# W_base turned and split during the attention periods and kept in DRAM, in a two-part transformer block on one core

## What is computed

```python
mod = (_silu(c) @ wmod).reshape(2, 6, 1, -1)
sa, ca, ga, sb, cb, gb = ...
h = layernorm(x) * (1 + ca) + sa
x = x + ga * attention(h, wq, wk, wv, wo)
h = layernorm(x) * (1 + cb) + sb
base = einsum('bsd,od->bso', h, W_base) + b_base
moe = experts(h, W_gate, W_thr, b_thr, A_w, B_w)
x = x + gb * (base + moe)
```

## Time and profile before

| | before |
|---|---|
| median of 3 runs | 1817.67 us |
| the profiled execution: time / span | 1819.76 / 1818.0 us |
| TensorE matmul busy | 1643.7 us (90%) |
| VectorE / ScalarE / GpSimd busy | 1010.9 / 985.4 / 611.1 us |
| mean DMA rate | 96 GB/s |
| chain that ended last: TensorE / ScalarE / VectorE / issue / DMA | 63 / 10 / 10 / 8 / 4% |

### The profile page before, as it was taken

How to read it: one execution, slowest core, us unless ns; L and a number is a source line. 1 busy time by engine, 2 the same in 40 slices (tenths; PEclk the granted TensorE clock), 3 DMA queues, 4 the chain that set the end, 5 groups by cost and what they waited for, 6 DMA issues and landing times.

```text
span 1818.0 us, 29711 instructions
## 1 busy us (share of the span) xinstructions
PE 1643.7 (90%) x9459; PEld 1196.8 (66%) x9459; DVE 1010.9 (56%) x3248; ACT 985.4 (54%) x2368; POOL 611.1 (34%) x483
## 2 busy tenths in 40 slices
PE   3667989999999998899999999999879999999997
PEld 0235666666666765677667667666457888888885
DVE  1535547667576664556666666665535445445443
ACT  1333667887887776667777777777742101101110
POOL 1441424334343230423433332331322333333342
PEclk8788999999999998999999999998589999999998
DMA  9633233444443338223323323223443211211210
GB/s 338 226 135 76 74 86 91 108 122 109 129 114 77 97 77 247 57 61 96 72 68 97 71 68 97 67 60 78 119 132 93 70 59 45 70 49 56 69 48 34
DMA packets 170786, 174.52 MB, mean 96 GB/s; under 512 B 20898, under 2 KB 120562, under 8 KB 170644
## 3 DMA queue, kind: packets, MB, share of 16 engines
q1 hardware_dynamic: 166484, 164.42, 32.5%
q10 hardware_dynamic: 4160, 8.39, 1.4%
HBM read 96.68 MB, written 25.21 MB: 67 GB/s over the span
## 4 chain that ended last, share of the span: by engine, by line
PE 63%; ACT 10%; DVE 10%; issue 8%; DMA 4%; POOL 3%; SPq 2%; ACTq 0%; DVEq 0%; POOLq 0%
PE ps_s L1186 12%; PE ps_s L661 10%; PE ps_qkv L1186 9%; PE ps_pv L1254 7%; PE ps_s L1229 7%; PE ps_t L1197 6%; ACT rows_sb L1436 4%; PE ps_s L622 3%; PE ps_s L623 3%; PE ps_s L624 3%; DVE rows_sb L1657 2%; ACT probsT L1472 1%; DVE bias_m L1675 1%; PE ps_qkv L663 1%; DVE ps_s L1698 1%
## 5 line engine op out<-in xcount | busy, mean ns | idle before, releaser
L1436 ACT ACTIVATE rows_sb<-rows_sb,bias_m 128x640 f32<-128x640 f32 (+7 forms) x512 | 398.1, 778 | 228.1 <-DVE bias_m L1675 227.8
L1657 DVE CUSTOM_DVE_ANT_0 rows_sb<-ps_t,mask 128x512 f32<-128x512 f32 (+3 forms) x512 | 296.8, 586 | 157.6 <-PE ps_t L1197 150.9
L1472 ACT ACTIVATE probsT<-ps_s 128x512 f32<-128x512 f32 (+2 forms) x640 | 321.5, 549 | 13.4 <-PE ps_s L1229 12.5
L1197 PE MATMUL ps_t<-stk 96*128 96x512 f32 (+3 forms) x768 | 277.5, 366 | 45.5 <-DVE m_rows L1688 25.7
L1229 PE MATMUL ps_s<-stk 98*128 98x512 f32 (+3 forms) x768 | 238.7, 392 | 16.2 <-DMA stk<-m_rows 12.0
L1698 DVE TENSOR_TENSOR ps_s<-ps_s,mask_t 128x128 f32<-128x128 f32 (+1 forms) x384 | 121.4, 340 | 184.5 <-PE ps_s L1229 182.8
L1197 PEld LDWEIGHTS ps_t<-stk 96*128 96x128 f32 x768 | 151.8, 198 | 102.8 <-DVE m_rows L1688 36.7
L1229 PEld LDWEIGHTS ps_s<-stk 98*128 98x128 f32 x768 | 135.9, 199 | 107.6 <-issue 51.9
L1254 PE MATMUL ps_pv<-probsT,v_all 128*32 128x256 f32 (+1 forms) x2816 | 189.3, 363 | 1.3 <-ACT probsT L1472 1.3
L1822 POOL TENSOR_TENSOR rope_b<-rope_b,rope_sin 128x512 f32<-128x512 f32 x64 | 82.2, 1284 | 278.0 <-DVE rope_b L1642 278.0
L1657 DVE CUSTOM_DVE_ANT_0 rows_sb<-ps_t,mask,smax_part 128x128 f32<-128x128 f32 (+3 forms) x256 | 140.8, 550 | 49.8 <-PE ps_t L1197 23.5
(11 more groups left out here) (190 smaller groups left out, 3085.9 us busy)
## 6 DMA issues: line engine op xcount, KB each, us to landing
stk<-rot SPq DMA_DIRECT2D x384, 128.0 KB, 2.4
probsT<-in_L_wmod_dram SPq DMA_DIRECT2D x5, 2048.0 KB, 8.3
wm_one<-in_L_wmod_dram SPq DMA_DIRECT2D x5, 2048.0 KB, 9.0
w_raw<-in_L_attn_wq_dram SPq DMA_DIRECT2D x16, 512.0 KB, 4.0
w_raw<-in_L_attn_wk_dram SPq DMA_DIRECT2D x16, 512.0 KB, 4.4
w_raw<-in_L_attn_wv_dram SPq DMA_DIRECT2D x16, 512.0 KB, 4.1
attn_scratch<-attn_sb SPq DMA_DIRECT2D x128, 64.0 KB, 3.1
a_raw<-attn_scratch SPq DMA_DIRECT2D x16, 512.0 KB, 4.9
```

The source lines that it names most:

```text
L1197: pe.matmul(bank[:, 0:c1 - c0], stk[0:3 * HD, u % 2, 0, qt // 4, h, qt % 4 * P:(qt % 4 + 1) * P], stk[0:3 * HD, u % 2, 1, part, h, 0:c1 - ...
L1436: act.activation(row, row, ACT.Exp, bias=bias_m[:, qt, h:h + 1], scale=SCALE, accum_out=sums[:, qt // 4, h, qt % 4:qt % 4 + 1]).then_inc(s ...
L1472: act.activation(probsT[:, w % 4, hs[0]:hs[-1] + 1, 0:n], s_bank[(NS * u + k) % 3][:, 0:len(hs) * n].rearrange("p (h n) -> p h n", h=len(hs)),
L1657: dve.tensor_tensor_reduce(rows_sb[:, to, at + c0:at + c1], bank[:, 0:n], mask[:, BANK - n:BANK] if last else mask[:, 0:1].broadcast_to([P ...
```

## The change

The split step gets 8 more tiles: in periods 10 to 17 the tile in x_next is a block of 128 rows of W_base. It takes no statistics, no norm and no modulation (one copy of 128x512 in place of four activations), and its halves are stored to wb_dram. At the end of period 30, SyncE waits for the last wo_lo and loads all of wb_lo from wb_dram (4 MB, one DMA); after the last scores matmul of period 31 it loads wb_hi (4 MB). W_base leaves `items`: the parts 0, 1 and 2 become one pass over three items, TensorE waits on wb_ld before the token tiles, and `load_early` loads three items.

```diff
-    if 0 <= u - LN_U < NT and i in NORM_STEPS:
+    if 0 <= u - LN_U < 2 * NT and i in NORM_STEPS and (u - LN_U < NT or NORM_STEPS[i][0] in ("turn", "split")):
         return u - LN_U, NORM_STEPS[i]
...
+    wb_dram = nc.dram_tensor("wb_scratch", [2, D, D], F32, kind="Internal").ap()
...
-        items = [("ag", 0), ("ag", 1), ("bt", 0)] + [("wb", o) for o in range(KT)]
+        items = [("ag", 0), ("ag", 1), ("bt", 0)]
...
-            for i in range(len(stage)):
+            for i in range(len(items)):
                 load_piece(sp, i)
...
-            load_pieces(range(len(stage), len(items)))
...
-            project(0, lambda: turn_weights(0))
-            turn_weights(1)
+            project(0, turn_weights)
 
             def rest_and_xn():
-                turn_weights(2)
                 pe.wait_ge(st_hi, UNITS)
                 pe.wait_ge(st_lo, UNITS)
                 turn_xn(0)
 
             project(1, rest_and_xn)
+            pe.wait_ge(wb_ld, 32)
             tile_loops(pe, body)
...
-                sp.dma_start(x_next[:, :], x_rows[n * P:(n + 1) * P, :]).then_inc(ln_x[tt % 2], 16)
+                rows = x_rows[n * P:(n + 1) * P, :] if tt < NT else W_base[(tt - NT) * P:(tt - NT + 1) * P, :]
+                sp.dma_start(x_next[:, :], rows).then_inc(ln_x[tt % 2], 16)
...
+            def load_wb(a, to):
+                sp.dma_start(to[:, :, :].bitcast(F32), wb_dram[a].rearrange("(k p) o -> p k o", p=P)).then_inc(wb_ld, 16)
...
-                if 0 <= u - 1 - LN_U < NT:
+                if 0 <= u - 1 - LN_U < 2 * NT:
                     store_next(u - 1 - LN_U, 1)
...
                 if u == PAIRS - 2:
                     load_a(sp, 0)
+                    sp.wait_ge(h_st, 2 * 16 * 4 * NT)
+                    sp.wait_ge(wo_lo_ok, KT)
+                    load_wb(1, wb_lo)
+            sp.wait_ge(st_ok, NS * PAIRS)
+            load_wb(0, wb_hi)
             store_attn(2 * PAIRS - 1)
             phase_b_sync(sp)
...
                 bank = ps_t[PLACE["ln", tt, half] % 2]
+                if tt >= NT:
+                    act.copy(h_next[:, :], bank[:, 0:BANK]).then_inc(h_mod[half], 1)
+                    return
```

More of the change, by code:

```diff
@@ L381, in adaln_block @@
         h_st = sem("h_st")
+        wb_ld = sem("wb_ld")
         hT_ld = [sem("hT_ld0"), sem("hT_ld1")]
@@ L487, in piece @@
             ks = slice(4 * half, 4 * half + 4)
-            if kind == "wb":
-                return tuple(w[:, ks, k * P:(k + 1) * P] for w in (wb_hi, wb_lo))
             if kind == "bt":
@@ L496, in piece_cols, with turned @@
             return AGW - ER if (kind, k) == ("ag", 1) else P
-        parts = [slice(0, 4), slice(4, 6), slice(6, len(items))]
         turn_bank = [ps_t[0], ps_t[1], ps_qkv, ps_pv]
-        def turned(part):
-            for i, (kind, k) in list(enumerate(items))[parts[part]]:
+        def turned():
+            for i, (kind, k) in enumerate(items):
                 for half in range(2):
@@ L532, in load_piece @@
             to, ld = stage[i % len(stage)], st_ld[i % len(stage)]
-            if kind == "wb":
-                sp.dma_start(to, W_base[k * P:(k + 1) * P, :]).then_inc(ld, 16)
-            elif kind == "bt":
+            if kind == "bt":
                 v = to.rearrange("p (t e r) -> p t e r", t=KT, e=E_)
@@ L559, in phase_b_sync @@
         def phase_b_sync(sp):
[L560 to L563, removed]
             def load_x(i, e):
@@ L603, in phase_b_tensor, with turn_weights @@
             pe.transpose(ps_pv[:, 0:4 * KT], mcol_rows[:, :], ident[0:4 * KT, 0:4 * KT]).then_inc(mcol2_t, 1)
-            def turn_weights(part):
-                for n, i, kind, k, half, bank in turned(part):
+            def turn_weights():
+                for n, i, kind, k, half, bank in turned():
                     if n == 0:
@@ L722, in body, with split_weights @@
                     split_h(i + 1)
-            def split_weights(part):
-                for n, i, kind, k, half, bank in turned(part):
+            def split_weights():
+                for n, i, kind, k, half, bank in turned():
                     rows = piece_cols(kind, k)
@@ L838, in body, with rest_weights @@
                     dve.tensor_tensor(x1[:, e, cols], x1[:, e, cols], xn[:, cols], ALU.add).then_inc(last_ok, 1)
-            def rest_weights(part):
-                for n, i, kind, k, half, bank in turned(part):
+            def rest_weights():
+                for n, i, kind, k, half, bank in turned():
                     rows = piece_cols(kind, k)
@@ L848, in phase_b_vector @@
             dve.wait_ge(wo_lo_ok, KT)
-            rest_weights(0)
+            rest_weights()
             dve.wait_ge(rows_ld, 16 * (B + 1))
@@ L954, in store_next @@
                 for a, part in enumerate((h_next_hi[:, :].bitcast(F32), h_next[:, :])):
-                    sp.dma_start(h_dram[a].rearrange("(k p) t -> p k t", p=P)[
-                        :, 4 * half:4 * half + 4, tt * P:(tt + 1) * P], part.rearrange("p (k t) -> p k t", k=4))\
+                    sp.dma_start((h_dram, wb_dram)[tt // NT][a].rearrange("(k p) t -> p k t", p=P)[
+                        :, 4 * half:4 * half + 4, tt % NT * P:(tt % NT + 1) * P], part.rearrange("p (k t) -> p k t", k=4))\
                         .then_inc(h_st, 16)
+            def load_wb(a, to):
+                sp.dma_start(to[:, :, :].bitcast(F32), wb_dram[a].rearrange("(k p) o -> p k o", p=P)).then_inc(wb_ld, 16)
             def load_w(j, t):
@@ L1073, in _ @@
                         load_wo(k)
-                if 0 <= u - LN_U < NT:
+                if 0 <= u - LN_U < 2 * NT:
                     store_next(u - LN_U, 0)
@@ L1092, in _ @@
                 store_attn(2 * u)
-                if 0 <= u + 1 - LN_U < NT:
+                if 0 <= u + 1 - LN_U < 2 * NT:
                     load_next(u + 1 - LN_U)
@@ L1128, in ln_half @@
                 n = b * NT + tt
-                pe.wait_ge(ln_xn, n + 1)
+                if tt < NT:
+                    pe.wait_ge(ln_xn, n + 1)
+                else:
+                    pe.wait_ge(ln_x[tt % 2], 16 * (NT // 2 + tt // 2 + 1))
                 x = x_next[:, :] if b else x_start[:, tt % 2, :]
```

6 lines of the change are left out of this document (1 added, 5 removed).

## The result

The changed kernel is slower: 1834.05 us in the median of 4 runs (1833.15 to 1835.77) against 1819.94 for the kernel before on the same chip, ratio 1.009 with a 95% interval of 1.0064 to 1.0116. So it costs 14 to 19 us; the forecast was 1840 against 1817.67, 22.

A forecast was written before the change was run, and what follows sets the result against it. TensorE's matmul time was taken as the bound (busy 1643.7 of 1818.0 us). Terms 12.8 + 9 + 11 + 2 - 11.2 + 0 - 1.3 = +22.3 gave 1842.1 by the profiled execution, 1840 for the median, range 1826 to 1852.

The forecast's parts named there:

- rival A: Only the last period waits; period 13's stores land in time or its loss is made up: 1831, chance 0.17.
- Part 1: Periods 10 to 17: eight split steps cost 1.6 us each, +12.8 us (3 to 26).
- Part 2: Period 13: ScalarE stands for h_next stores held behind the wv load, +9 us (0 to 12).
- Part 3: Period 31: m_rows wait behind the 4 MB wb_lo load, +11 us (0 to 18).
- Part 4: Period 31 behind the m_rows wait: TensorE resumes partly at half clock, +2 us.
- Rival B: Bulk loads don't hold short transfers or stores; parts 2 to 4 vanish: 1818, or 1808 with cheap steps; chance 0.12.
- Part 5: Start of the feed-forward part: eight W_base pieces no longer turned there, -11.2 us (-8 to -12).
- Part 6: After period 31's last scores: the 4 MB wb_hi load and transfers behind it cost 0 us (to +8).
- rival C: The 4 MB loads run at the hT loads' pace, 21.2 us, raising parts 3 and 6: 1855, chance 0.13.
- Part 7: Period 30: one early stage load fewer ahead of the last wo loads, -1.3 us (-1.7 to 0).

The follow-up runs named there:

- both executions of the changed kernel: The changed kernel, and the same kernel run again with no edit beside the kernel before; ratios 1.009 and 1.0094 to the kernel before.
- e7_short_first: Changed kernel with the wb_lo load behind m_rows and the wb_hi load behind a_raw, ga, bthr and x; 1825.28 us, ratio 1.0039.
- e4_both: Changed kernel with the wb_lo load behind m_rows and no split step in period 13; 1820.68 us, ratio 1.0021.
- e8_all_three: Changed kernel with period 13's store ahead of wv, wb_lo behind m_rows, wb_hi behind a_raw, ga, bthr and x; 1819.07 us, ratio 1.0004.
- e1_mrows_first: Changed kernel with only the 4 MB wb_lo load moved behind m_rows in SyncE's queue; 1828.99 us, ratio 1.0063.
- e5_steps_alone: Kernel before plus only the eight W_base split steps and their stores; 1839.49 us, ratio 1.0107.
- e10_five_pieces: As e8_all_three, but only the last five pieces of W_base turned in periods, with loads of 2.5 MB each; 1820.17 us, ratio 1.0006.
- e2_store_first: Changed kernel with period 13's two stores of h_next_hi and h_next ahead of the wv load; 1831.3 us, ratio 1.0081.

## Why the prediction was right, and where it was off

The direction held and so did the two waits behind larger transfers that carry most of it, and the time lies in the range. By the number alone rival A's 1831 is nearer to 1834.05 than the forecast's 1840; the traces decide between them. Several terms came near for reasons other than mine. Point by point:

**Part 1, the steps: +12.8 forecast, 11.5 by 8 x 1.44**, with 1.44 measured in periods 16 and 17. The size is right, but its working isn't. I added 8.6 and 5.2 us of the earlier trace rows to 1.7 us of waiting per period. These are the same eight waits seen twice, once by the weight load and once by the matmul that starts with it, as here in the order of time of the kernel before:

```profile
362.50 0.19 PEld L1197 LDWEIGHTS ps_t<-stk 96*128 96x128 f32 x1 [0.90 <-ACT h_next L1374]
362.50 0.33 PE L1197 MATMUL ps_t<-stk 96*128 96x128 f32 x1 [0.46 <-ACT h_next L1374]
```

TensorE's matmuls stood 5.2 / 8 = 0.65 us per period for it, not 1.7. That TensorE's own 1.39 us stays didn't hold either: a step of W_base added 0.94 us of busy time and 0.50 of standing, where one of x had added 1.39 and 1.83. The two errors nearly cancel, which is luck. Of the 1.33 us of standing that went, the wait for h_next explains at most 0.65; the rest no run separates.

**Part 2, period 13: +9 forecast for the stand, 8.3 measured, but 5.4 to 5.8 net.** Periods 13 to 15 grew by 9.7 and 10.1 us, of which three steps are 4.3. This is the term that was mis-sized most, by some 3.4 us. The stand was read rightly, and it is paid in full: taking 6.7 of its 8.3 us away gained 7 us on these periods. The step of the prediction that failed is the sum behind it, which takes part 1 and part 2 as if period 14 stayed as it was. In both executions of the changed kernel period 14 ran at full or nearly full clock and took 1.4 to 1.6 us less than before with its own step of 1.44 in it: 2.9 to 3.0 us that I had not in the sum. It isn't a fixed discount: in e7_short_first, with the same step and the same stand, it failed to come, and periods 13 to 15 grew by 12.9 us, 8.6 net of the steps, close to my 9.

**Part 3, m_rows: +11 forecast, 10.0 measured.** I took 14 us for 4 MB; it took 13.0. Rival B, that short transfers pass the bulk, is out: 11.81 us in the same queue, and even in another one 5.15.

**Part 4, the clock: +2 forecast, 2.9 and 2.3 measured** (period 31 grew by 12.88 and 12.32 to its last copy, less the 10.0). The size is right, but that the wait causes it isn't shown. The view by stretch before the wait, in it, and behind it in two parts:

```profile
core 0: us, PE busy (x) PEld busy (x) DVE busy (x) ACT busy (x) POOL busy (x), PEclk, DMA share, GB/s
1329.20:1341.36 12.16, 5.23 (x35) 2.86 (x35) 2.19 (x5) 7.48 (x14) 5.02 (x3) 0.50 0.63 177
1341.36:1351.67 10.31, 0.01 (x1) 0.00 (x0) 0.43 (x1) 0.38 (x1) 2.02 (x1) 0.50 0.97 382
1351.67:1359.85 8.18, 8.18 (x38) 3.92 (x38) 0.25 (x1) 4.62 (x9) 0.00 (x0) 0.50 0.08 18
1359.85:1365.27 5.42, 4.38 (x51) 1.98 (x50) 1.64 (x6) 2.88 (x7) 0.00 (x0) 1.00 0.06 8
```

The clock was at its 1.2 GHz level 12 us before TensorE began to stand, and for 8.2 us after it resumed, then at 2.4 GHz: of the stretch behind the wait neither all nor nothing ran at half clock. From the first matmul behind m_rows to the last attention copy it is 10.75 us before, 13.60 and 13.39 in the changed kernel. With no such wait it is 10.72 to 10.74 in e4_both, e7_short_first and e8_all_three, but 13.39 to 13.43 in e1_mrows_first, e5_steps_alone and e10_five_pieces. With a wait of 2.5 us or more (seven traces) it was never under 13.09. So the wait may keep the clock down, but the same 2.7 us are also lost without it, and period 31 of e5_steps_alone, where nothing is held, took 3.7 us more than before.

**Part 5, the start: -11.2 forecast, -12.6 and -11.1 measured.** Parts 3 to 5 were to make +1.8 together and made +0.3 and +1.2.

**Part 6, wb_hi: 0, right, with little to spare.** VectorE stood 5.85 us for bthr and began xn at 1383.95, 1.22 us long; a_lo, for which TensorE waited, ended at 1385.54. With m_rows freed xn was the later one, and 1.9 us were lost. I had priced the transfers behind wb_hi only for a slower bulk (rival C), not for two bulks in a row.

**Part 7, an early load fewer: -1.3 forecast, -2.65 and -0.69 measured** over periods 29 and 30.

With these the sum is 11.5 + 5.6 + 0.8 - 1.7 = +16 in place of +22.3, between the +14 and +19 of the two comparisons. It leaves out what no part names, such as 2 us in periods 18 to 28 in both executions. Of the 6 us between, part 2 is 3.4, part 1 1.3, parts 3 to 5 another 1.0 and part 7 0.4. Rival A (1831), that nothing is lost in period 13 or that it is made up, was right by a third of the stand in the changed kernel, through the clock of period 14. How far the first comparison lies under the second is not explained by the kernel; it is within their intervals.

## What to carry to other kernels

A load of megabytes put into a queue is charged to whatever small transfer comes behind it: list what the queue issues in the next 15 us and who waits for it, and put the bulk behind those, as late as its own reader allows. Here that order alone was worth 16 us by the ratios (1.0094 to 1.0004), the whole loss of the change. Freeing one transfer leaves the next one in the queue behind the bulk, so move all bulks before judging a move. And work that is moved off a serial stretch into a full one costs its own engine time there: 11.5 us paid for some 12 saved is no gain, however well the waits are hidden.

## What the runs showed that I had not expected

In periods with no change between the kernels, the granted clock falls to half for a few us now and then, in other periods from execution to execution: period 22 took 34.11 us at 1.00 before and 36.18 at 0.95 in the changed kernel, TensorE being busy for over 32 us in both. Each such spell costs some 2 us: periods 16 and 17, 70.24 us at 1.00, took 72.23 at 0.98 in e2_store_first and e5_steps_alone. Over periods 2 to 28 without 13 the half clock sums to 26.0 us before, 20.4 in the changed kernel and 34.6 in its second execution. Some two or three spells more or less are as large as the difference between two runs of one kernel, and differences of 2 to 4 us between variants stayed open with 6 to 12 runs each. What sets off such a spell, no run here shows.
